# Six-head graph attention on one core: scores and context side by side, softmax one slot later, another prologue

## What is computed

```python
h = jnp.maximum(_layernorm(x, axis=-1), 0.0)
scores = jnp.einsum('bhqd,bhkd->bhqk', q, k) / np.sqrt(HEAD_SIZE)
bias = jnp.where(graph_mask, 0.0, NEG)[:, None]
ctx = jnp.einsum('bhqk,bhkd->bhqd', jax.nn.softmax(scores + bias, axis=-1), v)
x = x + (ctx.reshape(B, S, H) @ Wf + bf)
```

## Time and profile before

| what | value |
|---|---|
| median of 3 runs | 1002.41 us |
| the profiled execution, its own time | 1000.85 us |
| its span | 999.0 us (1.85 us lie around it) |
| PE busy | 95% of the span, granted clock 0.99 |
| DVE, ACT, POOL busy | 84%, 78%, 67% |
| DMA queue | 60% of 16 engines' span |
| loads of the four weights | 576 KB each, 4.3 to 7.3 us to landing |

### The profile page before, as it was taken

One profiled execution on the slowest core, in us unless ns is written; L12 is line 12 of the kernel. 1 busy time (PEld: TensorE's weight loads), 2 busy tenths in 40 slices (PEclk: granted clock), 3 DMA queues, 4 the chain that ended last, 5 costly groups with the idle time before them and its releaser, 6 DMA issues.

```text
span 999.0 us, 28223 instructions
## 1 busy us (share of the span) xinstructions
PE 948.1 (95%) x8649; PEld 510.8 (51%) x8649; DVE 838.4 (84%) x1621; ACT 780.8 (78%) x2373; POOL 670.3 (67%) x1163
## 2 busy tenths in 40 slices
PE   1889999999999999999999999999999999999976
PEld 0445555555555555555555555555555555555543
DVE  4688888888888888898888888888889888888774
ACT  3687788888878888888888887888888888888663
POOL 4676677777776767767777677776776777777431
PEclk9999999999999999999999999999999999999997
DMA  7447656566566565655656656656565565666454
GB/s 199 75 90 152 123 126 141 127 139 147 130 135 136 129 140 130 148 133 126 141 127 141 145 130 133 138 129 139 132 148 133 124 143 128 140 146 121 92 94 90
DMA packets 359834, 130.86 MB, mean 131 GB/s; under 512 B 325376, under 2 KB 359808, under 8 KB 359808
## 3 DMA queue, kind: packets, MB, share of 16 engines
q1 hardware_dynamic: 359808, 130.54, 60.4%
HBM read 29.82 MB, written 25.17 MB: 55 GB/s over the span
## 4 chain that ended last, share of the span: by engine, by line
issue 44%; POOL 41%; PE 5%; ACT 2%; POOLq 2%; DVE 2%; DMA 2%; SPq 0%; DVEq 0%; ACTq 0%
POOL x_bias L807 13%; POOL s L816 11%; POOL rstd L775 7%; POOL mask L786 3%; POOL shift L778 2%; POOL rstd L770 2%; PE ps_qk L301 2%; POOL shift L772 2%; DMA pt<-parts 2%; POOL h_parts L795 1%; POOLq L165 1%; PE ps_v L301 1%; PE ps_r L301 1%; ACT s L473 1%; DVE s L650 1%
## 5 line engine op out<-in xcount | busy, mean ns | idle before, releaser
L473 ACT ACTIVATE s<-s,neg_max 128x128 f32<-128x128 f32 x768 | 297.7, 390 | 53.3 <-DVE neg_max L664 53.3
L816 POOL TENSOR_TENSOR s<-s,inv_sums 128x384 f32<-128x384 f32 x256 | 212.2, 829 | 132.7 <-DVE inv_sums L639 132.7
L795 POOL TENSOR_TENSOR h_parts<-h,h_parts 128x384 f16<-128x384 f32 x128 | 121.3, 948 | 146.1 <-ACT h_parts L515 146.1
L301 PE MATMUL ps_v<-w_hi_v,ht 128*128 128x384 f16 x768 | 209.4, 328 | 0.0
L301 PE MATMUL ps_qk<-ht,w_hi_q 128*128 128x512 f16 x576 | 172.5, 381 | 3.6 <-DVE w_lo_q L545 3.3
L301 PE MATMUL ps_qk<-ht,w_hi_k 128*128 128x512 f16 x576 | 171.3, 379 | 0.0
L807 POOL TENSOR_TENSOR x_bias<-x_in,out_bias 128x384 f32<-128x384 f32 x128 | 170.1, 1329 | 0.4
L494 ACT ACTIVATE parts<-s 128x768 f16<-128x768 f32 x128 | 107.3, 838 | 55.0 <-POOL s L816 55.0
L650 DVE SCALAR_TENSOR_TENSOR s<-ps_s,unscale,mask 128x384 f32<-128x384 f32 x256 | 145.2, 609 | 1.0
L473 ACT ACTIVATION_READ_ACCUMULATOR s<-s,neg_max 128x1 f32 x768 | 145.5, 189 | 0.0
L301 PE MATMUL ps_r<-w_hi_f,ct_hi 128*128 128x384 f16 x384 | 128.2, 334 | 14.3 <-DVE ct_lo L688 13.1
(11 more groups left out here) (77 smaller groups left out, 1806.6 us busy)
## 6 DMA issues: line engine op xcount, KB each, us to landing
x_in<-in_x SPq DMA_DIRECT2D x128, 192.0 KB, 2.9
out<-y SPq DMA_DIRECT2D x128, 192.0 KB, 2.1
ht<-h_parts SPq DMA_TRANSPOSE x128, 2.9
adj_in<-in_adj SPq DMA_DIRECT2D x32, 64.0 KB, 2.7
pt<-parts SPq DMA_TRANSPOSE x128, 3.7
w_raw_f<-in_L_gnn_Wf SPq DMA_DIRECT2D x1, 576.0 KB, 5.2
w_raw_q<-in_L_gnn_Wq SPq DMA_DIRECT2D x1, 576.0 KB, 6.2
w_raw_v<-in_L_gnn_Wv SPq DMA_DIRECT2D x1, 576.0 KB, 7.3
```

Source lines behind the costliest of these rows:

```text
L301: last = mm(psum, parts_a[a](i), parts_b[b](i), start=n == 0, stop=n == len(todo) - 1)
L473: last = activation(s[:, b, hd, :], s[:, b, hd, :], ACT.Exp, bias=neg_max[:, b, hd:hd + 1], accum_out=sums[:, b, hd:hd + 1])
L795: nc.gpsimd.tensor_tensor(h_parts[:, b, 1, :], h[:, b, :], h_parts[:, b, 0, :], ALU.subtract).then_inc(h_lo_ready, 1)
L816: nc.gpsimd.tensor_tensor(s[:, b, half, :], s[:, b, half, :], inv_sums[:, b, half].unsqueeze(2).to_broadcast([128, PAIRS, NODES]), ALU.mul ...
```

## The change

- PE's order is projection, q/k tile, scores, context, values, second q/k tile; in slots with j = 0 it is projection, values, scores, context, two q/k tiles. Scores and context now stand next to each other.
- Exponentials, reciprocals and `normalised` of graph t move from slot t to t+1, the transpose from t+1 to t+2, the context from t+2 to t+3, projection, residual and store from t+3 to t+4. `pt` gets four buffers.
- Values are projected one slot ahead of their graph's scores (VALUES = 1) and not four.
- ACT and DVE have an order of their own for j = 0, for j = 2 and for short slots. On POOL `x_bias` goes last. SP stores before it turns h.
- Prologue: weights are loaded q, k, v, f right after each other; the scales are made one slot earlier; w_lo of v and f are made in slots -2 and -1; POOL makes the lower half of h one slot later, until slot 0.

```diff
...
-LOAD, STATS, NORM, TURN, LATE = 11, 10, 9, 8, 3
-XB = 4
+LOAD, STATS, NORM, TURN, LATE = 11, 10, 9, 8, 4
+XB, VALUES = 4, 1
...
-pt = sb("pt", [128, 2, 2 * HEADS, NODES], F16)
+pt = sb("pt", [128, 4, 2 * HEADS, NODES], F16)
...
-        if t == 1 - LOAD:
-            with nc.allow_non_contiguous_dma(reason="a bias vector, once"):
-                sp.dma_start(bv_col[:, :], column(bv)).then_inc(bv_loaded, 16)
-            load_weight("f", Wf)
         if t == 2 - LOAD:
             load_weight("q", Wq)
+            load_weight("k", Wk)
         if t == 3 - LOAD:
             load_weight("v", Wv)
-        if t == 4 - LOAD:
-            load_x(3)
-            load_weight("k", Wk)
+            load_weight("f", Wf)
             with nc.allow_non_contiguous_dma(reason="bias vectors, once"):
+                sp.dma_start(bv_col[:, :], column(bv)).then_inc(bv_loaded, 16)
...
-            for u in range(4, RING):
-                load_x(u)
...
         if isinstance(t, int):
             wait(sp, h_lo_ready, u + 1)
+            wait(sp, v_ps, t + VALUES)
             if ju == 0:
-                wait(sp, v_ps, t + GROUP)
+                wait(sp, qk_ps, 2 * (t + GROUP))
...
-        if k % GROUP != 0:
-            turn_h(t, k)

...
-        if k % GROUP == 0:
-            turn_h(t, k)
-
-        if valid(t - 1):
-            b = (k - 1) % 2
+        turn_h(t, k)
+
+        if valid(t - 2):
+            u, b = t - 2, k % 2
...
+                wait(sp, parts_lo, u + 1)
+            sp.dma_start_transpose(pt[:, (k - 2) % 4, :, :], parts[:, b, :, :].rearrange("p a n -> p (a n)")
...
     def weights(t):
-        if t == -5:
+        if t == -6:
             pe.wait_ge(largest_ready, 1)
             nc.tensor.transpose(ps_s[0:4, 1, 0:128], largest[:, :], ident[:, :]).then_inc(largest_ps, 1)
-        if t == -4:
+        if t == -5:
...
             if start:
-                wait(pe, w_lo_ready, 1 + 2 * tile)
+                wait(pe, w_lo_ready, 1 + tile)
...
-        def v_tile():
...
+        def v_tile(u, ku):
+
+            if not valid(u):
...
+            pu, ju = group_of(u, ku)
+            if isinstance(t, int) and u == 0:
+                wait(pe, w_lo_ready, 3)
+            wait(pe, v_ready, u - 1)
...
-        scores(t, k)
-        projection(t - 3)
-        qk_tile(tiles[0])
-        context(t - 2, k - 2)
-        v_tile()
+        projection(t - 4)
+        if j == 0:
+            v_tile(t + VALUES, k + VALUES)
+            scores(t, k)
+            context(t - 3, k - 3)
+            qk_tile(tiles[0])
+        else:
+            qk_tile(tiles[0])
+            scores(t, k)
+            context(t - 3, k - 3)
+            v_tile(t + VALUES, k + VALUES)
         if two:
             qk_tile(tiles[1])
...
     def weights(t):
-        if t == -4:
+        if t == -5:
             upper_weights()
...
-            if not project:
-                return
...
+            u = t + VALUES
+            if not valid(u):
...
+            wait(act, v_ps, u + 1)
...
         def exponentials(odd):

-            if not valid(t):
-                return
-            b = k % 2
+            u, b = t - 1, (k - 1) % 2
+            if not valid(u):
+                return
...
-            u = t - 2
+            u = t - 3
...
-        else:
-            upper_probs()
+        elif isinstance(t, int) and t < 0:
+            qk_tile(tiles[0])
             norm()
-            upper_h()
-            exponentials(0)
-            qk_tile(tiles[0])
-            context()
-            exponentials(1)
-            v_tile()
             if two:
                 qk_tile(tiles[1])
+            upper_h()
+            v_tile()
+        else:
+            if j == 0:
+                exponentials(0)
+                exponentials(1)
+                norm()
+                upper_h()
+                context()
+                qk_tile(tiles[0])
+                qk_tile(tiles[1])
+                v_tile()
+                upper_probs()
+            elif j == 2:
+                exponentials(0)
+                exponentials(1)
+                norm()
+                context()
+                upper_h()
+                v_tile()
+                qk_tile(tiles[0])
+                qk_tile(tiles[1])
+                upper_probs()
+            else:
+                exponentials(0)
+                norm()
+                context()
+                upper_h()
+                qk_tile(tiles[0])
+                exponentials(1)
+                v_tile()
+                upper_probs()
...
     def weights(t):
-        if t in (-9, -8, -7, -6):
-            largest_of({-9: "f", -8: "q", -7: "v", -6: "k"}[t])
+        if t in (-8, -7):
+            largest_of("qk"[t + 8])
         if t == -6:
+            largest_of("v")
+            largest_of("f")
...
         if t == -5:
             common_power()
+            scales()
+        if t == -4:
+            low_weights("qk")
+            output_bias()
+        if t == -2:
+            low_weights("v")
+        if t == -1:
+            low_weights("f")
...
         def reciprocals(odd):

-            if not valid(t):
+            u, b = t - 1, (k - 1) % 2
...
+            if not valid(t - 3):
+                return
+            wait(dve, ct_hi_ready, t - 2)
...
-            wait(dve, ct_ps, u - 1)
...
-        else:
-            if isinstance(t, int) and t == -GROUP:
-                scales()
-                low_weights("qvkf")
-                output_bias()
-            masked_scores(t, k)
-            maxima(t, k)
-            lower_probs()
+        elif isinstance(t, int) and t < 0:
             spread()
-            residual()
-            if valid(t + STATS):
-                dve.wait_ge(bn_done, t + STATS + 1)
-            reciprocals(0)
+            dve.wait_ge(bn_done, t + STATS + 1)
+            mean_and_variance()
             qk_lower(PROJECTED[j][0])
-            mean_and_variance()
-            lower_context()
-            reciprocals(1)
-            lower_v()
             if len(PROJECTED[j]) == 2:
                 qk_lower(PROJECTED[j][1])
+            lower_v()
+        else:
+            if j == 0:
+                residual()
+                masked_scores(t, k)
+                reciprocals(0)
+                lower_context()
+                reciprocals(1)
+                spread()
+                qk_lower(PROJECTED[j][0])
+                maxima(t, k)
+                if valid(t + STATS):
+                    dve.wait_ge(bn_done, t + STATS + 1)
+                lower_v()
+                mean_and_variance()
+                lower_probs()
+                qk_lower(PROJECTED[j][1])
+            elif j == 2:
+                residual()
+                reciprocals(0)
+                reciprocals(1)
+                masked_scores(t, k)
+                lower_context()
+                lower_v()
+                spread()
+                qk_lower(PROJECTED[j][0])
+                if valid(t + STATS):
+                    dve.wait_ge(bn_done, t + STATS + 1)
+                qk_lower(PROJECTED[j][1])
+                mean_and_variance()
+                maxima(t, k)
+                lower_probs()
+            else:
+                residual()
+                reciprocals(0)
+                lower_context()
+                masked_scores(t, k)
+                reciprocals(1)
+                qk_lower(PROJECTED[j][0])
+                maxima(t, k)
+                spread()
+                if valid(t + STATS):
+                    dve.wait_ge(bn_done, t + STATS + 1)
+                lower_v()
+                mean_and_variance()
+                lower_probs()
...
-        def lower_h():
-
-            u, b = t + NORM, (k + NORM) % 2
+        def lower_h(u, ku):
...
         def normalised(odd):

-            if not valid(t):
-                return
-            b, half = k % 2, slice(odd * PAIRS, (odd + 1) * PAIRS)
-            wait(pool, inv_ready, 2 * t + 1 + odd)
+            u, b, half = t - 1, (k - 1) % 2, slice(odd * PAIRS, (odd + 1) * PAIRS)
+            if not valid(u):
+                return
+            wait(pool, inv_ready, 2 * u + 1 + odd)
...
+        if isinstance(t, int) and t < 0:
+            factors()
+            lower_h(t + NORM - 1, k + NORM - 1)
+            mask_of_next()
+            biased_x()
+            return
+        if isinstance(t, int) and t == 0:
+            lower_h(t + NORM - 1, k + NORM - 1)
         factors()
         mask_of_next()
-        lower_h()
-        biased_x()
+        lower_h(t + NORM, k + NORM)
         normalised(0)
         normalised(1)
+        biased_x()
```

More of the change, by code:

```diff
@@ L260, in slot @@
                                  ).then_inc(adj_loaded[at], 16)
-                if valid(t + LOAD) and not (isinstance(t, int) and 3 <= t + LOAD < RING):
+                if valid(t + LOAD):
                     u, r = t + LOAD, (k + LOAD) % RING
@@ L275, in slot @@
                                  ).then_inc(stored[r], 16)
-                if k % GROUP == 0:
```

(59 more changed lines are left out.)

17 lines of the change are left out of this document (7 added, 10 removed).

## The result

The changed kernel takes 1028.62 us (median of 4 runs, 1025.93 to 1029.37), the one before 1001.99 in the same comparison: ratio 1.026, interval 1.0247 to 1.0271. It is slower; the forecast was 973.5 and faster. The profiled execution has a span of 1027.6 us.

The account below looks back on a forecast made before the run. The prediction took PE's own time to bound the steady part. From the profiled 1000.85 us it summed - 12.4 - 9 - 2.4 + 3.7 - 4.4 - 3 = 973.35, given as 973.5, range 960 to 991.

Parts of the forecast that it names:

- (a): PE, scores next to context: three form changes a slot instead of four, 0.10 each over 124 slots, -12.4 us.
- R2: Rival: PE's step from scores to context is free, giving 961 us; chance 0.08.
- R3: Rival: scores and context side by side save nothing on PE, giving 986 us; chance 0.08.
- (b): Steady part: most of PE's 10.4 us of stalls go, as ACT's and DVE's order follows PE's; -9 us.
- R1: Rival: the context's halves are late in short slots, mass between 982 and 1000 us; chance 0.19.
- R4: Rival: the loop of POOL and ACT becomes the bound, slower, up to 1037 us; chance 0.05.
- (c): Softmax, context and projection one slot later: half of PE's idle time in the first slots comes back, -2.4 us.
- (e): Values one slot ahead: three value tiles move from the prologue into PE's idle time in the drain, -4.4 us.
- (f): Prologue: scales and upper halves come one slot earlier, first tile at 24, -3 us (-6 to 0).
- (d): Drain: the last graph passes one slot more, its transpose behind a store awaiting a projection; +3.7 us (1 to 6).
- (g): Moved issues of h turns and x loads, dropped waits and four `pt` buffers: no cost.

Follow-up runs that it names:

- e7: e2 with scores and context apart again, so four form changes a slot instead of three: 993.7 us, ratio to before 0.992.
- e2: Changed kernel with DVE's statistics of x (spread, mean and variance) moved right behind the residual or the masked scores: 976.79 us.
- e8: e2 with SP issuing the transpose of the probabilities ahead of the store from slot 125 on: 977.75 us.
- e1: Changed kernel with ACT's copy of the context's upper half ahead of norm in every slot: 1020.2 us.
- e3: Changed kernel with the edits of e1 and e2 together: 1002.88 us.
- e4: Changed kernel with POOL's x_bias back ahead of the two normalised, as before the change: 1026.32 us.
- e11: e2's kernel again, unchanged, in five runs: 980.55 us, ratio to before 0.977.
- e9: Changed kernel with DVE's lower_probs ahead of the mean and variance in short slots and j = 0: 1049.23 us.

## Why the prediction was wrong

**(a) Right.** The step from scores to context is 0.09 in the median of 125 steps, a slot has three changes, and e7 prices the fourth at 0.09 to 0.10. R2 and R3 are out. The Trainium skill, TensorEngine Tiling (Array Packing), Key Properties, says that a change of the tiling mode drains TensorE; the trace agrees, by this 0.09.

**(b) Wrong, and this is the step that failed.** "In my walk ACT and DVE are both waiting when the short slot's context ends, since DVE has 6.55 and ACT 6.10 us of work to 7.2 of PE." They were waiting, but for each other. The 1.34 from context to projection was read in the tail, where no `norm` and no statistics are left. In the steady part the copy stands behind `norm`, which waits for POOL's factors, which wait for DVE's `moments`, near the end of its slot. I had taken a wait that goes round for idle time to spare. In place of -9 the term is +38: after's 7.610 a slot stands against the 7.19 that term (a) gives without stalls (7.29 - 0.10), which is 0.42 a slot or 48.7 us of stalls, where before had 10.4. Moving DVE's statistics alone takes the slot to 7.220 (e2). The argument against R1, "long slots give the lag back", fails for the same reason: the turns that go with long slots are 8.27 and 7.94. Of the 56.0 us between the sum, 973.35, and the profiled 1029.37, this term has 47.3, the first slots 6.6 and the drain 1.8. A small slip is in the forecast too: the sum starts from the profiled execution, so the median forecast should have been 1.6 above it, 975 and not 973.5.

**R4 had the kind of mechanism and not the place.** It gave a loop through POOL and ACT, with the copy `ct_hi` in it, of 6.88 against a limit of 7.18 and a chance of 0.05. The turns that go through POOL and ACT alone bear it out: 7.22 and 7.15 in after, 6.95 and 6.96 in e2. What its sum lacked is DVE. In every second turn the loop passes through DVE's slot up to `moments`: POOL waits for them 52.0 us in after, and in the kernel before it did not wait (no idle time before its first factor). And the collision lay elsewhere: I placed it on `x_bias`, whose mean fell from 1361 to 1003 ns, while the first two factors rose from 192 and 191 to 674 and 384. Summed over the loop that is a gain of 0.36 and a loss of 0.68. The sign R4 named, PE waiting for q/k halves, is there, though as the smaller part. The point from which R4 decides, the mean slot of 7.18, held: 7.645 in after is above it and costs, 7.185 in e2 is at it and does not. The sign of my chances, 0.92 faster, rests on "several parts that don't hang together"; they did hang together, through (b).

**(c), (e), (f) Right in part.** The first tile starts at 23.48 (forecast 24) and the first scores at 39.23 (forecast near 40), against 27.05 and 46.14 before. So (e) and (f) came as forecast. Of these 6.9 us only 3.2 are left at graph 8; in e2, 8.8 are. So the first slots lose their gain to the same order of DVE, and (c), half of 4.7, shows up only in e2 (1.9 more at graph 8 than at the first scores).

**(d) Within its bounds, open in cause.** 44.1 us against 38.6 is +5.5, and +3.8 in e2, where I gave +3.7 (1 to 6). But e8 takes away the store ahead of the transpose, which was my reason, and gains nothing measurable. The waits point elsewhere too: in the drain PE waits 3.7 us for `pt` (before: 5.9) and 11.6 for `ct_lo` (before: 7.0). That the size fits is luck as far as the reason goes; what sets the drain stays open.

**(g)** Moved DMA issues: between 150 and 930 us PE waits for `pt` once in e2, for 1.2 us, and in after not at all. Right for this kernel; e1, e3 and e4 (20 to 36 us) show how little it takes to lose that.

So the forecast, 973.5, is 3 to 7 us below what the same change does with DVE's statistics in another place: 976.79 in e2's run, 980.55 in e11's median. One order of small operations decided between 0.977 and 1.026.

## What to carry to other kernels

When several engines run in a fixed order, idle time of an engine is no slack until it is known what it waits for. Write out, per kind of slot, the loop that goes from one engine's operation through the others back to it, with each operation that stands in order ahead of a link. Then add the turns up over a whole period of slots and compare that with the bounding engine's work in the same slots: 30.58 against 28.76 lost time here, and 28.74 against 28.76 did not, though no turn fitted into the shortest slot in either. An operation that others wait for, above all a short one, goes where its own engine was going to wait anyway; moving 0.7 us of work made the difference between 1028.6 and 980.6 us here.

## What was not expected of the hardware

A [128 x 1] operation of POOL, 0.19 us alone (190 ns in e9), took 0.81 when it began 0.17 us after DVE's subtract of two SBUF tiles (513.69, 0.93 long) and ended with it. The Trainium skill, SBUF — State Buffer, Who interferes with whom, says that GpSimd shares its ports with DVE's second pair as an exclusive lock; the trace agrees, and adds that the short operation pays for the whole length of the long one. In e2 the collision is not gone: L839 takes 535 ns in the mean and L842 844, and the four factors add up to 1.78 us against 1.80 in after. It costs e2 nothing that shows, since PE sets the pace there.

A change between the form with 64 rows and the one with 64 columns costs the same 0.09 to 0.10 us as one between either and the full array.
